# Inverse roots and sigmoids from exponentials and logarithms in a two-layer AdaLN kernel

## The reference

```python
mod = (silu(L_c) @ L_wmod).reshape(8, 6, 1, -1)       # sa, ca, ga, sb, cb, gb
h = layernorm(x) * (1 + ca) + sa;  x = x + ga * attn(h)
h = layernorm(x) * (1 + cb) + sb;  x = x + gb * ffn(h)
```

```python
lr = sigmoid(xk @ theta + tb);  eta = token_eta * lr / 64
Z1 = xk @ W + b;  x_hat = (Z1 - mean) / sqrt(var + eps)      # then a gradient, dW, Wn = W - dW
Zq = xq @ Wn + bn;  out = xq + g * (Zq - mean) / sqrt(var + eps) + beta
```

## Time and profile before

| | |
|---|---|
| median of three runs | 1000.49 us (999.88 to 1000.78) |
| span of the profiled execution | 996.6 us; its own time outside the profile is not recorded, the runs' median is 3.9 us longer than the span |
| busy: TensorE, VectorE, ScalarE, GpSimd | 932.1, 792.1, 659.4, 332.9 us |
| mean granted clock of TensorE | 0.973 of full |
| instructions | 27072 |

### The profile page before, as it was taken

One profiled execution on the slowest core, in us unless ns is written; L12 is line 12 of the kernel. 1 busy time (PEld: TensorE's weight loads), 2 busy tenths in 40 slices (PEclk: granted clock), 3 DMA queues, 4 the chain that ended last, 5 costly groups with the idle time before them and its releaser, 6 DMA issues.

```text
span 996.6 us, 27072 instructions
## 1 busy us (share of the span) xinstructions
PE 932.1 (94%) x10930; PEld 710.6 (71%) x10930; DVE 792.1 (79%) x1953; ACT 659.4 (66%) x1246; POOL 332.9 (33%) x434
## 2 busy tenths in 40 slices
PE   6689899999999989899999999999999998999995
PEld 5566476777777776677778776677878766777772
DVE  3845549987989778997789869897888968888873
ACT  2363346689666576698756576699766567786772
POOL 1970002225241421224342322233442334455451
PEclk9689989999999999999999999999999999999998
DMA  9000010000000010000000010000000000000000
GB/s 330 14 2 1 1 43 2 2 2 2 3 1 2 13 44 1 2 2 2 2 13 1 12 33 12 1 3 2 3 12 2 10 14 13 1 4 12 3 2 21
DMA packets 15831, 16.03 MB, mean 16 GB/s; under 512 B 2013, under 2 KB 14301, under 8 KB 15325
## 3 DMA queue, kind: packets, MB, share of 16 engines
q1 hardware_dynamic: 15709, 14.31, 4.7%
HBM read 10.12 MB, written 2.10 MB: 12 GB/s over the span
## 4 chain that ended last, share of the span: by engine, by line
PE 65%; DVE 22%; ACT 6%; issue 3%; POOL 3%; DMA 1%; ACTq 0%; SPq 0%; DVEq 0%; POOLq 0%
PE ps L532 8%; PE ps L589 5%; PE ps L595 4%; PE ps L613 4%; PE ps L525 4%; PE ps L583 4%; PE ps L572 4%; PE ps L514 3%; PE ps L481 3%; PE ps L472 3%; PE ps L398 2%; PE ps L507 2%; DVE tmp L1111 2%; POOL gbase L1312 2%; DVE tmp L1116 2%
## 5 line engine op out<-in xcount | busy, mean ns | idle before, releaser
L1312 POOL TENSOR_TENSOR gbase<-zhat,gamma 128x512 f32<-128x512 f32 x64 | 81.7, 1276 | 320.6 <-DVE scl L1105 313.1
L1320 POOL TENSOR_TENSOR zq_sqq<-zq_sqq,qinv 128x512 f32<-128x512 f32 x64 | 67.9, 1063 | 260.9 <-DVE qinv L1128 254.7
L589 PEld LDWEIGHTS ps<-grad,k_sc 64*65 64x65 f32 x2048 | 67.2, 137 | 25.0 <-issue 22.9
L772 ACT COPY w_sb<-ps 65x1024 f32<-65x1024 f32 x66 | 66.4, 1007 | 24.7 <-PE ps L589 23.6
L532 PEld LDWEIGHTS ps<-w_sb,keys 65*64 65x64 f32 x2048 | 65.6, 138 | 21.7 <-issue 12.6
L532 PE MATMUL ps<-w_sb,keys 65*64 65x64 f32 x2048 | 73.1, 224 | 6.4 <-ACT keys L780 4.8
L589 PE MATMUL ps<-grad,k_sc 64*65 64x64 f32 x2048 | 74.9, 223 | 4.2 <-DVE grad L1122 4.0
L532 PEld LDWEIGHTS ps<-w_sb,queries 65*64 65x64 f32 x2048 | 65.1, 138 | 15.2 <-issue 10.0
L532 PE MATMUL ps<-w_sb,queries 65*64 65x64 f32 x2048 | 72.6, 224 | 2.7 <-issue 1.7
L595 PEld LDWEIGHTS ps<-h,pack_ttt 128*128 128x128 f32 x512 | 64.2, 195 | 11.3 <-issue 6.4
L595 PE MATMUL ps<-h,pack_ttt 128*128 128x128 f32 x512 | 70.7, 283 | 0.2 <-ACT k_tok L800 0.2
(11 more groups left out here) (244 smaller groups left out, 2346.7 us busy)
## 6 DMA issues: line engine op xcount, KB each, us to landing
x<-in_x SPq DMA_DIRECT2D x8, 256.0 KB, 3.5
xc<-x SPq DMA_DIRECT2D x16, 128.0 KB, 2.4
out_x<-xc SPq DMA_DIRECT2D x16, 128.0 KB, 2.4
pack_ttt<-in_ttt SPq DMA_DIRECT2D x1, 1216.0 KB
keys<-in_gam_bet_rows SPq DMA_DIRECT2D x1, 1024.0 KB
w_sb<-in_compose SPq DMA_DIRECT2D x1, 1024.0 KB, 9.3
zq_sqq<-in_wmod SPq DMA_DIRECT2D x1, 768.0 KB, 4.9
pack_expert<-in_expert SPq DMA_DIRECT2D x1, 680.0 KB, 16.0
```

The source lines that it names most:

```text
L589: last = mm(bank[2 * f + c][0:C, h * HD:(h + 1) * HD], k_sc[64 * c:64 * c + 64, HH * f + h, :], grad[64 * c:64 * c + 64, h, :], start=Fals ...
L772: nc.scalar.copy(w_sb[:, f, :, :, :].rearrange("p b h d -> p (b h d)"), ps[0:C, 2 * f:2 * f + 2, :].rearrange("p a c -> p (a c)")).then_in ...
L1312: P.tensor_tensor(gbase[:, cols], zhat[:, cols], gamma2[:, cols], ALU.mult).then_inc(S["g_hat"], 1)
L1320: P.tensor_tensor(heads(zq_hat[:, cols]), heads(zq_hat[:, cols]), per_head(qinv[:, hs]), ALU.mult).then_inc(S["zq_ready"], 1)
```

## The change

Each inverse root becomes two ScalarE instructions, exp(-0.5 * ln(scale * x + eps)) in `inverse_root`, and VectorE's reciprocals of roots go, with the letter `y` on VectorE. GpSimd's scaling now waits for ScalarE. The sigmoids of silu and rates become exp(-x) on ScalarE with a lower bound on x before it, and an addition and a reciprocal after it, on VectorE. The mixing's sigmoid becomes a lower bound on VectorE (which drains the bank, in MIX_IN) and exp(-ln(1 + exp(-x))) in three ScalarE instructions, in MIX_OUT. One table set is named at the start of ScalarE's program. All orders and the sequence of banks are new; `WARM` is not changed. Of the orders the diff below shows the first line (for ScalarE and VectorE also the last); renamed buffers and semaphores are left out.

```diff
--- before.py
+++ after.py
@@ -29,6 +29,7 @@
 HALF = HH * HD
 C = HD + 1
 EPS_K, LN_EPS, TTT_EPS = 1e-4, 1e-5, 1e-6
+SIG_LEAST, LOG_LEAST = -80.0, -44.0
 NORM = DH ** -0.25
 ROOT_HD = 8.0
 
@@ -86,38 +87,37 @@
 ORDERS = {
-    "PE": ("110011011010001110011011001010100110111000100010rkslkqa00lsbqa0110dkklbea11dleakb1q0dlbfkefla0dqkqea10bolkff1bdoqaekld"
...
+    "PE": ("101011010110100110011011001010110010011100100010rkslkqa00lsb1qa010dklbeak1d1laekb1q0ldbkfefa0lqdqke1a0bolfkf1ob0dqe1al"
...
-    "ACT": ("001110110010110011100111011000010111100100010010r1k0slka0vlsqqa0v1dkklae1vwdleavk11wq00ldkfefalvdqqewawkv0olff111dokqe"
...
-            "aewvodfqfewdefwmmfoommmmmm"),
+    "ACT": ("1011010110100010111101010100100101111001000010100rkslk1a0vlsqqa0v1kdleka1wv1dl0aevkw1q0dlkfefalvqdqewakw0olfvf111odqka"
...
+            "wawvofdmqefwdewomffmommmmm"),
-    "DVE": ("111110001001001100111111000000111110011000001100r1001azbca0z0bcea1z1yazbecy0bc0a1zee1yay0bcz1bcaze11yebaycz111bc00aze1"
...
-            "emmbcayzebcyeayzbceymeymmmmmmm"),
+    "DVE": ("10110110100011011100101101000101011100001001110000r1az1bca0z0bcea1z1aezbc0bc0ae1ze1a0bcz11bcaez11eba10zcbc10eaz001bc0a"
...
+            "zebaczebcazebcamzebcaezbcazebcamzebmacezbcazebcazebcazbecamzmbecazbecaezbcememmmmmmm"),
-BANKS = ("0123456710235467315607312546073461072534610725436071254360721543607215436027154360271543675467674567565764576746754654"
...
+BANKS = ("0123456702345167405627430510621706243157062431570624315706243157062431570642315706423157645764674657656754675745674674"
...
...
         def _(act):
+            nc.scalar.preload_act_table_set("natural_log_exp_and_others")
             loaded(act, "mod")
-            nc.scalar.activation(s_sig[:, :, :], cT, ACT.Sigmoid).then_inc(act_set, 1)
-            def root(name, src, dst, u=None, scale=1.0, eps=LN_EPS):
...
-                key = name if u is None else f"{name}_{u}"
-                nc.scalar.activation(dst, src, ACT.Sqrt, bias=eps, scale=scale).then_inc(S[key], 1)
+            act.wait_ge(set_step, 1)
+            nc.scalar.activation(s_sig[:, :, :], s_sig[:, :, :], ACT.Exp, scale=-1.0).then_inc(act_set, 1)
+            logs = [0]
...
+            def inverse_root(src, log, dst, sem, scale=1.0, eps=LN_EPS):
...
+                nc.scalar.activation(log, src, ACT.Ln, bias=eps, scale=scale).then_inc(S["logged"], 1)
+                logs[0] += 1
+                act.wait_ge(S["logged"], logs[0])
+                nc.scalar.activation(dst, log, ACT.Exp, scale=-0.5).then_inc(sem, 1)
...
                 act.wait_ge(S[f"ln1_var_{u}"], 1)
-                root("ln1_std", L[u]["mv"][:, :, 1], L[u]["std"][:, :], u)
+                inverse_root(L[u]["mv"][:, :, 1], L[u]["log"][:, :], L[u]["inv"][:, :], S[f"ln1_inv_{u}"])
...
                     act.wait_ge(S[f"{name}_var_{u}"], p + 1)
-                    root(f"{name}_std", l["mv"][:, :, 1], l["std"][:, :], u)
+                    inverse_root(l["mv"][:, :, 1], l["log"][:, :], l["inv"][:, :], S[f"{name}_inv_{u}"])
...
             def start(p):
-                ready(act, f"rate_{p}")
-                nc.scalar.activation(eta[:, :, :], eta[:, :, :], ACT.Sigmoid).then_inc(S["rate_sig"], 1)
+                act.wait_ge(S["rate_bounded"], p + 1)
+                nc.scalar.activation(eta[:, :, :], eta[:, :, :], ACT.Exp, scale=-1.0).then_inc(S["rate_sig"], 1)
...
                     act.wait_ge(S["z_var"], g + 1)
-                    nc.scalar.activation(zstd[:, hs], ssum[:, hs], ACT.Sqrt, bias=TTT_EPS * HD).then_inc(S["z_std"], 1)
+                    if g >= 2:
+                        act.wait_ge(S["scale_ready"], g - 1)
+                    inverse_root(ssum[:, hs], zlog[:, hs], zinv[:, hs], S["z_inv"], eps=TTT_EPS * HD)
...
                     act.wait_ge(S["zq_var"], g + 1)
-                    nc.scalar.activation(qstd[:, hs], qsum[:, hs], ACT.Sqrt, bias=TTT_EPS, scale=1.0 / HD).then_inc(S["zq_std"], 1)
+                    if g >= 2:
+                        act.wait_ge(S["zq_ready"], g - 1)
+                    inverse_root(qsum[:, hs], qlog[:, hs], qinv[:, hs], S["zq_inv"], scale=1.0 / HD, eps=TTT_EPS)
...
                     act.wait_ge(S["ln6_var"], n + 1)
-                    nc.scalar.activation(std6[:, :], mv6[:, :, 1], ACT.Sqrt, bias=LN_EPS).then_inc(S["ln6_std"], 1)
+                    inverse_root(mv6[:, :, 1], log6[:, :], inv6[:, :], S["ln6_inv"])
...
                     nc.scalar.activation(kact, kact, ACT.Square).then_inc(S["key_ready"], 1)
-                    src = filled(act, f"r_{n}")
-                    nc.scalar.activation(r_sb, src, ACT.Sigmoid).then_inc(drained(f"r_{n}"), 1)
+                elif step == MIX_OUT:
+                    ready(act, f"r_{n}")
+                    nc.scalar.activation(r_sb, r_sb, ACT.Exp, scale=-1.0).then_inc(S["r_step"], 1)
+                    act.wait_ge(S["r_step"], 2 * n + 1)
+                    nc.scalar.activation(r_sb, r_sb, ACT.Ln, bias=1.0).then_inc(S["r_step"], 1)
+                    act.wait_ge(S["r_step"], 2 * n + 2)
+                    nc.scalar.activation(r_sb, r_sb, ACT.Exp, scale=-1.0).then_inc(S["r_done"], 1)
...
                 l = L[u]
-                dve.wait_ge(S[f"{name}_std_{u}"], p + 1)
-                link(V.reciprocal(l["inv"][:, :], l["std"][:, :]))
+                dve.wait_ge(S[f"{name}_inv_{u}"], p + 1)
...
             loaded(dve, "mod")
+            link0(V.tensor_scalar(s_sig[:, :, :], cT, SIG_LEAST, None, ALU.max))
             dve.wait_ge(act_set, 1)
+            link0(V.tensor_scalar(s_sig[:, :, :], s_sig[:, :, :], 1.0, None, ALU.add))
+            link0(V.reciprocal(s_sig[:, :, :], s_sig[:, :, :]))
...
                     for t in range(T):
-                        V.scalar_tensor_tensor(l["y"][:, t, :], l["y"][:, t, :], l["mv"][:, t, 0:1], gg3[:, u, 0, :], ALU.subtract, ALU.mult)
-                    dve.wait_ge(S[f"ln3_std_{u}"], p + 1)
-                    link(V.reciprocal(l["inv"][:, :], l["std"][:, :]))
+                        n = go_on(V.scalar_tensor_tensor(l["y"][:, t, :], l["y"][:, t, :], l["mv"][:, t, 0:1], gg3[:, u, 0, :], ALU.subtract, ALU.mult))
+                    settled(n)
+                    dve.wait_ge(S[f"ln3_inv_{u}"], p + 1)
...
                 elif what == "z":
-                    dve.wait_ge(S["z_std"], g + 1)
-                    link(V.reciprocal(zinv[:, hs], zstd[:, hs]))
+                    dve.wait_ge(S["z_inv"], g + 1)
...
                     V.tensor_reduce(qsum[:, hs], heads(sqq), AX, ALU.add).then_inc(S["zq_var"], 1)
-                elif what == "y":
-                    dve.wait_ge(S["zq_std"], g + 1)
-                    V.reciprocal(qinv[:, hs], qstd[:, hs]).then_inc(S["zq_inv"], 1)
...
                 V.tensor_tensor(eta[:, :, :], src, bc_tb[:, :].unsqueeze(1).broadcast_to([128, NJ, H]), ALU.add).then_inc(drained(f"rate_{p}"), 1)
+                ready(dve, f"rate_{p}")
+                V.tensor_scalar(eta[:, :, :], eta[:, :, :], SIG_LEAST, None, ALU.max).then_inc(S["rate_bounded"], 1)
                 dve.wait_ge(S["rate_sig"], p + 1)
+                link(V.tensor_scalar(eta[:, :, :], eta[:, :, :], 1.0, None, ALU.add))
+                link(V.reciprocal(eta[:, :, :], eta[:, :, :]))
...
                 elif step == MIX_NORM:
-                    dve.wait_ge(S["ln6_std"], n + 1)
-                    link(V.reciprocal(inv6[:, :], std6[:, :]))
+                    dve.wait_ge(S["ln6_inv"], n + 1)
...
                     V.scalar_tensor_tensor(mix_r[:, :], diff_flat, mu_r[:, :], h4_flat, ALU.mult, ALU.add).then_inc(S["mix_ready"], 1)
+                elif step == MIX_IN:
+                    dve.wait_ge(S["mix_ready"], 2 * n + 2)
+                    V.tensor_scalar(r_sb, filled(dve, f"r_{n}"), LOG_LEAST, None, ALU.max).then_inc(drained(f"r_{n}"), 1)
                 elif step == MIX_OUT:
-                    dve.wait_ge(S["mix_ready"], 2 * n + 2)
-                    ready(dve, f"r_{n}")
+                    dve.wait_ge(S["r_done"], n + 1)
```

More of the change, by code:

```diff
@@ new lines @@
+    "DVE": ("10110110100011011100101101000101011100001001110000r1az1bca0z0bcea1z1aezbc0bc0ae1ze1a0bcz11bcaez11eba10zcbc10eaz001bc0a"
+            "ez0b1c1az0bcae0ezbm1cazm00b0c0eeaz101b10aczebca001e1z1bce0me1m10r1mm0amz1bca0z0bca1z1ebcaez1bceamz01a0ebzc10bc111ae0zm"
+            "b1ca1ez1bca0z010ebc1azb10ce0eaz0bc0ea0zbcmea0z0b0ca0zem1b10c1e0amzbc1az0b1ec1me0e11m1r001azabmzmc00mbcea1z1bcaze0bcae0"
+            "z1e1abzcb10a1e1mczb1cmaze11b0c001az1be0cea0z0b1cea0zbc0aez0bcmazm00b1ec01eaz01bc0ae01mz1bce1az0bc0me1e11ramzbcmazmbcam"
+            "zebaczebcazebcamzebcaezbcazebcamzebmacezbcazebcazebcazbecamzmbecazbecaezbcememmmmmmm"),
@@ L137, in turns @@
     assert all(n in (0, PAIRS * PER_TOKEN[what]) for what, n in taken.items()), taken
-PER_BATCH = [f"ln{n}_{what}" for n in range(1, 6) for what in ("var", "std", "hat")]
+PER_BATCH = [f"ln{n}_{what}" for n in range(1, 6) for what in ("var", "inv", "hat")]
```

(13 more changed lines are left out.)

50 lines of the change are left out of this document (23 added, 27 removed).

## The result

The changed kernel takes 1034.15 us, median of 4 runs, against 1000.63 us for the kernel before on the same chip: ratio 1.0394, 95% interval 1.0312 to 1.0477. Forecast was 988.7 us, range 977 to 1001. It is 33.5 us slower by the medians where 12 us faster was forecast. The ratio, estimated from the single runs, stands for 39 us.

What follows compares the result with a forecast made beforehand. TensorE, busy 932.1 of 996.6 us, was taken as the bound, so gains could come only from stretches where it idles. Terms summed to -11.8 us: 984.8, plus 3.9 around the span, 988.7; range 977 to 1001.

Steps and rivals of the forecast that it cites:

- the one on the roots: All 176 roots: latency unchanged to 0.02 us; ScalarE gains 37 us of work, VectorE loses 33.
- the sum: Gains added over the kernel's stretches, start to tail: -11.8 us in all, 984.8 against a span of 996.6.
- Neither becomes the bound: Engine totals: ScalarE goes from 659 to 666 us busy, VectorE from 792 to 768; neither limits the kernel.
- The slower rival: In the slots, new orders and banks make TensorE wait; 0.5 us per slot gives 1009 us; chance 0.10.
- its break-even of 0.19: In the slower rival, a TensorE wait of 0.19 us per slot (12/64) cancels the forecast gain.
- Start, -4: 0 to 150 us: reordered first work of both batches sums to -5.1 us, taken as -4 for possible collisions.
- the forecast's 50: In the start, batch 1's context matmuls were to begin at about 50 us instead of 54.8.
- Loads, about -7.8 with the reciprocals: Stretches after the start, through the tail: -0.7, -2.9, -1.2, -1.5, 0 and -1.5 us from fewer loads and reciprocals.
- this case: Eight table loads on the chain each save 1.38 us of drain too: 11.0 us more, 978; chance 0.01.
- Last pair, 0: 826 to 965 us: the chain keeps its 8.19 us per slot, so no gain; bounds +2 and -3.

Runs made afterwards that it cites:

- e5: e1 with VectorE copying the readout's inverse root at the old reciprocal places and GpSimd's scaling waiting for that copy; 1.0070 of the kernel before.
- e7: Kernel before without VectorE's reciprocal of the readout's root, GpSimd waiting for ScalarE alone; 1.0076 of the kernel before.
- e11: Changed kernel with GpSimd's three big scalings of a slot cut from 512 to 8 columns from the third slot on; 1.0057 of the kernel before.
- e13: e1 with GpSimd's three big scalings of a slot cut from 512 to 8 columns; 1.0001 of the kernel before.
- e1: Changed kernel's new functions under the old orders and banks, mixing's lower bound on VectorE left out; 1.0153 of the kernel before.
- e17: Changed kernel without GpSimd's small copy in each slot, VectorE writing its scale straight into k_sc's last column; 1.0427 of the kernel before.
- e4: e1 with the new orders and banks for the first 48 steps of layer 0; 1.0148 of the kernel before.
- e10: Kernel before without 32 of its 33 table loads, square roots and sigmoids replaced by other single functions; 0.9952 of the kernel before.
- e6: e5 with mixing's r computed by one activation instead of three; 1.0047 of the kernel before.
- e12: Kernel before with GpSimd's three big scalings of a slot cut from 512 to 8 columns; 0.9888 of the kernel before.

## Why the prediction was wrong

- **The step that failed** is the one on the roots: "a root's chain is unchanged to 0.02 us. What changes is who is occupied". The latency was right: Ln 0.21, gap 0.03, Exp 0.21 in the changed kernel. But the readout's reciprocal was also GpSimd's release, and its place in VectorE's order kept GpSimd off the steps that read only SBUF. I costed 64 reciprocals as 12.5 us of VectorE saved; they were worth 8 us of the kernel's time by being there (e5 and e7, from both sides).
- **The larger part of the miss** is a term that the sum put at nothing: what the new orders and banks cost in the slots. Every row of the sum gives them a gain or 0, with the durations of the kernel before. The runs show 24 us (18 by the medians), of which all but 6 go when GpSimd's three scalings are cut (e11, e13). How they cost it stays open. It is not more stretch of the four steps, which sum to 195.0 us under the new orders and 193.7 under the old (e1).
- **"Neither becomes the bound"**: 768 us of VectorE assumed that every duration stays and that each reciprocal taken away frees its whole length. It was 800. Before, the reciprocals lay partly beside VectorE's next instruction (954.25 + 0.20 against 954.36 in the rows above): without them the trace of before has 772.1 us of VectorE busy, 20 less and not 33. That is 13 of the 32. Stretch on the four SBUF steps is 195.0 - 184.5 = 10.5; layer norm steps that read SBUF are longer as well (the mixing's hat step 479 ns instead of 342). The rates' reciprocal took 0.95 us and not 0.29, 2 more.
- **The slower rival** (new orders and banks make TensorE wait, 0.10) had the side right. Its sum is wrong as it stands: 0.5 us in each of 64 slots is 32 us and gives 1021, not 1009. Measured is 24 us, 0.38 a slot, twice its break-even of 0.19. Its mechanism, a bank whose reader comes late, is not shown: with GpSimd's scalings cut the same orders and banks cost 6. Whether it is the scalings' length or what they lie beside that does it was not told apart; e17 speaks against 0.4 us of length being enough.
- **Start, -4**: 5.8 us ahead at slot 0, of which about 3 at a like clock, spent by slot 15 (+2.4 against before). By e4 it is not worth anything at the end. The context matmuls of batch 1 start at 47.42, earlier than the forecast's 50, and those of batch 0 at 53.92 (60.41 before).
- **Loads, about -7.8 with the reciprocals**: the loads alone were worth 4.8 us (e10), of 41.1 us of ScalarE. Here the order of size was right. By the Trainium skill, "ScalarE: Activation LUTs", "Table sets", Ln and Exp share a table; the one load left agrees. The same page, "What ACT_TABLE_LOAD costs", states a drain of 1.38 us beside each load, an estimated 11.0 us for the eight loads on the chain. The interval of e10's whole gain ends at 7.7 us, so this case does not bear that out.
- **Last pair, 0**: the period of plain slots stayed at 8.2 (944.88 to 953.07 in gbase's starts), as forecast; the 9 us that the pair lost lie in slots with mixing and attended chunks on GpSimd, such as 961.26 to 972.36 (11.1 us, 8.4 before).
- **Functions, open part**: with the say given back and mixing at one activation, the new functions still cost 5 us (e6, 1 to 9); with GpSimd cut 11 (e13 against e12). The clock does not explain e6, whose runs had a mean of 0.971 against 0.969 before; e13's had 0.972 against e12's 0.977, which can be a part of the 11. Whether the second activation of each root takes the rest was not tested under the old orders.

## What to carry to other kernels

An instruction of 0.2 us whose result releases another engine is also that engine's clock: before you delete it or hand it on, ask what the released engine will now run beside. Where VectorE and GpSimd share SBUF work, cost a new order with their overlaps, not with single durations, since an order planned from single durations can lose what it seems to win. To find who carries a loss, cut one engine's instructions to a few columns in both kernels and compare the differences of the medians.

## What was not expected of the hardware

- VectorE instructions with all big operands in SBUF go from 0.69 up to 1.65 us beside a GpSimd scaling, GpSimd's readout scaling from 1.04 up to 1.59; reductions (0.67) and steps with an operand in PSUM (0.69) do not change beside the same work. The Trainium skill, "SBUF — State Buffer", section "SBUF: two separate sides", says that the two engines share one pair of ports, which a VectorE instruction with two SBUF inputs or a GpSimd instruction holds to its end. The traces agree in which instructions lengthen; I had not weighed it in the prediction.
- The runs of one kernel spread with TensorE's clock. The kernel before took 990.5 us in a run with a mean granted clock of 0.981 and 1002.7 in one with 0.965. The clock falls to 0.50, the level of 1.2 GHz, in stretches behind a short idle, not each time. In e6, behind a wait for k_tok at the last seam that TensorE also has in the kernel before (0.77 us in both), rows of e6, then before:

```profile
820.00:825.00 5.00, 4.23 (x26) 2.99 (x27) 1.08 (x4) 2.84 (x7) 0.00 (x0) 0.79 0.00 0
825.00:830.00 5.00, 5.00 (x47) 4.66 (x46) 3.29 (x6) 1.76 (x3) 0.00 (x0) 0.50 0.01 3
830.00:835.00 5.00, 5.00 (x17) 2.88 (x17) 1.92 (x5) 2.52 (x6) 2.40 (x3) 0.68 0.23 52
```

```profile
815.00:830.00 15.00, 13.19 (x106) 9.62 (x105) 6.47 (x13) 13.01 (x21) 2.91 (x4) 1.00 0.08 19
830.00:845.00 15.00, 12.20 (x224) 9.63 (x224) 13.41 (x33) 9.71 (x21) 5.48 (x8) 1.00 0.01 2
```

So a difference of several us between two profiles of such kernels can go with the clock alone (e12's start was 7.5 us faster over the same instructions), and medians over runs decide.
